# Keys and queries stored by feature with their norms folded, four unread matmuls per step, and the 64 recurrence steps written out

## The reference, cut to what matters

```
q, k, v = x@Wq, x@Wk, x@Wv            # x after a layer norm; 8 heads of 64
beta, tg = sigmoid(x@Wbeta), sigmoid(x@Wtg)   # per head and mode
qr = l2norm(rotary(q, cos, sin)) * 64**-0.5
kr = l2norm(rotary(k, cos, sin))      # angles differ by head and mode
g  = log(clip(tg * rho, 1e-6))
def step(S, inp):                     # over 512 tokens, all m, b, h
    S  = S * exp(g_t)
    dv = (v_t - k_t @ S) * beta_t
    S  = S + outer(k_t, dv)
    return S, q_t @ S
o = sum over m of softmax(mode_logits) * ys
x = x + (o * sigmoid(x@Wg)) @ Wo
x = x + experts(layernorm(x))
```

## Time and profile before

| | |
|---|---|
| median of 3 runs | 4784.18 us (4780.45 to 4792.02) |
| profiled execution, its own time | 4793.02 us |
| its span | 4790.8 us |
| mean granted TensorE clock | 0.873 of full |
| PE busy, share of the span | 4015.4 us, 84% |
| PEld | 3307.7 us, 69% |
| DVE | 3652.5 us, 76% |
| ACT | 2902.2 us, 61% |
| POOL | 371.3 us, 8% |
| DMA | 314.77 MB, mean 66 GB/s |

### The profile page before, as it was taken

One profiled execution on the slowest core, in us unless ns is written; L12 is line 12 of the kernel. 1 busy time (PEld: TensorE's weight loads), 2 busy tenths in 40 slices (PEclk: granted clock), 3 DMA queues, 4 the chain that ended last, 5 costly groups with the idle time before them and its releaser, 6 DMA issues. The chain is left out here.

```text
span 4790.8 us, 195228 instructions
## 1 busy us (share of the span) xinstructions
PE 4015.4 (84%) x85713; PEld 3307.7 (69%) x85713; DVE 3652.5 (76%) x7742; ACT 2902.2 (61%) x9736; POOL 371.3 (8%) x156
## 2 busy tenths in 40 slices
PE   5502999889988998889889988898899889987999
PEld 2201777777777777777777777777777777775666
DVE  6754888778877887788778877887788778854655
ACT  5742666666666666666666666666566666654443
POOL 1221000000000000000000000000000000000000
PEclk8755889889888998899889988998899889988999
DMA  4675222322232223222322231223122312203110
GB/s 119 167 182 133 52 51 56 83 53 52 52 87 53 52 52 87 53 52 52 87 53 52 52 87 47 57 52 87 40 59 58 82 44 58 57 10 83 36 31 7
DMA packets 283082, 314.77 MB, mean 66 GB/s; under 512 B 135768, under 2 KB 182752, under 8 KB 278112
## 3 DMA queue, kind: packets, MB, share of 16 engines
q1 hardware_dynamic: 282208, 301.99, 26.7%
HBM read 232.70 MB, written 69.21 MB: 63 GB/s over the span
## 5 line engine op out<-in xcount | busy, mean ns | idle before, releaser
L926 DVE TENSOR_TENSOR run_SC<-run_SP,run_DB 128x512 f32<-128x512 f32 x512 | 350.1, 687 | 474.6 <-PE run_SP L1057 468.3
L943 DVE TENSOR_TENSOR run_XL<-run_XL,run_EL 128x30 f32<-128x30 f32 (+14 forms) x1920 | 637.3, 332 | 66.0
L942 DVE TENSOR_TENSOR run_EL<-run_AL,run_XL 128x30 f32<-128x30 f32 (+14 forms) x1920 | 636.7, 332 | 66.0
L1053 PE MATMUL run_SP<-run_KP 64*32 64x128 f32 x8192 | 624.8, 302 | 24.5 <-DVE run_KP L901 12.7
L980 POOL TENSOR_TENSOR run_DB<-run_DB,run_below 128x2048 f32<-128x2048 f32 x64 | 297.9, 4655 | 3613.7 <-DVE run_XL L943 3487.9
L801 ACT ACTIVATE run_DB<-run_DB,run_col 128x64 f32<-128x64 f32 x2048 | 537.3, 337 | 12.0 <-POOL run_DB L980 4.2
L1053 PEld LDWEIGHTS run_SP<-run_KP 64*32 64x32 f32 x8192 | 465.6, 119 | 101.8 <-issue 50.0
L859 ACT COPY run_S<-run_KS 128x256 f32<-128x256 f32 x448 | 166.9, 373 | 556.5 <-PE run_KS L1118 556.5
L808 ACT ACTIVATE run_KD<-run_PR,run_col 128x64 f32<-128x64 f32 x2048 | 471.6, 327 | 12.9 <-PE run_PR L1073 6.8
L846 ACT ACTIVATE run_R<-run_KS,run_col 128x64 f32<-128x64 f32 x1792 | 416.0, 323 | 102.8 <-PE run_KS L1082 102.4
L1057 PE MATMUL run_SP<-run_KP 64*32 64x64 f32 x8192 | 454.5, 243 | 0.0
(11 more groups left out here) (201 smaller groups left out, 7588.8 us busy)
## 6 DMA issues: line engine op xcount, KB each, us to landing
run_DB<-G_s SPq DMA_DIRECT2D x256, 256.0 KB
run_EG<-EG_s SPq DMA_DIRECT2D x128, 512.0 KB, 8.9
run_tab<-TAB_s SPq DMA_DIRECT2D x128, 256.0 KB, 10.5
KQ_s<-proj_win SPq DMA_DIRECT2D x32, 768.0 KB, 7.8
run_win<-KQ_s SPq DMA_DIRECT2D x64, 384.0 KB, 3.1
TAB_s<-tab_tab SPq DMA_DIRECT2D x128, 128.0 KB, 2.4
run_V<-V_s SPq DMA_DIRECT2D x128, 128.0 KB, 2.6
V_s<-proj_vv SPq DMA_DIRECT2D x64, 128.0 KB, 3.1
```

The costliest lines, as they stand in the source:

```text
L942: v.link(dve.tensor_tensor(e, bcast(AL[:, r + 1:, r], 2, done), bcast(XL[:, r, 0:done], 1, rows), ALU.mult))
L943: less = dve.tensor_tensor(XL[:, r + 1:, 0:done], XL[:, r + 1:, 0:done], e, ALU.subtract)
L1053: pe.matmul(out[64 * e:64 * e + C, p].rearrange("p (z u) i -> p z (u i)", z=2), KP[f, par, p, t0:t1], KP[f, kq, p, t0:t0 + SPAN], start=Tr ...
```

## The change

**Project.** PE multiplies Wk and Wq (now the stationary operand, 128 features at a time) by all 512 tokens, so features lie on partitions. `KQ_s` holds them unscaled, by feature, with a plane for z = keys and one for queries; the rotation's negated half comes from a third product with `wn`, the negated weights. Squares are summed on PE against `pair`, two columns of ones. Instead of scaling the keys, V is multiplied by the key's norm (`root`) and the term of beta by its square; the queries' inverse norm goes to `RQ_s`, and the experts multiply the outputs by it. POOL has nothing left to do here. Each sequence's `KQ_s` is stored by 16 DMAs (before: 4), and there is one more for `RQ_s`.

**Recurrence.** `load_kq` loads `kqT` straight from `KQ_s` by 6 DMAs (1 MB) once the rotation of the pair before is done; `transposes`, `transposed`, `win` and `pe_t`, `act_t` are gone. `token_keys` uses both banks in turn. `stay_busy` is a 128x256 matmul of `ident` by `Sdec` into a half of a bank that nothing reads before it is written anew: two stand before merge(0, 0) (not in the first step), one between merge(0, 0) and merge(0, 1), and one before merge(1, 0). The tables of places move the last three token_keys one place forward and spread ACT's key copies. All 64 steps are one `emit` with constant addresses; there is no loop and no barrier within them.

**Experts.** One more DVE multiplication of 128x512 per tile of 128 tokens, 32 in all, before the one by the gate.

```diff
@@ project, store of keys and queries
-                    for i in range(NT):
-                        sp.dma_start(KQ_s[:, b, :, i, :].rearrange("h p e -> p h e"), win[:, i, :, :]).then_inc(put_k, 16)
+                    for h in range(H):
+                        at, of4 = 64 * (h % 2), 32 * (h % 4)
+                        sp.dma_start(KQ_s[h, b, :, 0:DK].rearrange("z f t -> f z t"), kf[at:at + 64, b % 2, :, h // 2, :]).then_inc(put_k[b % 2], 16)
+                        sp.dma_start(KQ_s[h, b, :, DK:].rearrange("z f t -> f z t"), nf[of4:of4 + 32, b % 2, :, h // 4, :]).then_inc(put_k[b % 2], 16)
@@ project, the products on PE
-                    pe.matmul(QB[n % 2][:, :], lhsT, wq[:, :], start=True, stop=True).then_inc(pe_q, 1)
+                    for query, w in enumerate((wk, wq)):
+                        if n:
+                            pe.wait_ge(freed[query], n)
+                        pe.matmul(FB[query][:, :], w[:, 128 * i:128 * i + 128], xT[:, b % 2], start=True, stop=True).then_inc(pe_f[query], 1)
@@ recurrence, SP
-                            sp.wait_ge(scored, SUPER * k + 2)
-                            if k + sets:
-                                sp.wait_ge(pe_t, 4 * (k + sets))
-                            load_win(n)
+                            sp.wait_ge(rot_k, NT * (k + 1))
+                            sp.wait_ge(rot_q, NT * (k + 1))
+                            load_kq(n)
@@ recurrence, merge
                             if m == 0 and k:
                                 pe.wait_ge(xt_done, 2 * k - 1)
-                                if g == 0:
-                                    pe.wait_ge(kd_done, SUPER * k)
-                                else:
-                                    pe.wait_ge(act_t, 4 * turned)
+                                pe.wait_ge(kd_done, SUPER * k)
@@ recurrence, PE
+                        def stay_busy():
+
+                            pe.matmul(KS[:, 0].rearrange("p a v -> p (a v)"), ident[:, :], Sdec[:, :, :].rearrange("p a v -> p (a v)"),
+                                      start=True, stop=True)
+
                         if runs:
+                            if k:
+                                stay_busy()
+                                stay_busy()
                             merge(0, 0)
+                            stay_busy()
                             merge(0, 1)
+                            stay_busy()
                             merge(1, 0)
-                            jobs = sc[0:1] + jobs + sc[1:] + kd[0:2] + turn[0:2] + kd[2:3] + turn[2:3] + kd[3:4] + turn[3:4]
+                            jobs = sc[0:1] + jobs + sc[1:] + kd
@@ recurrence, the order and the loop
-        PE_PLACES = [1, 2, 1, 1, 2, 1, 1, 1, 0, 0, 1, 1, 1, 1, 1, 1]
-        ACT_PLACES = [1, 1, 1, 1, 1, 1, 0, 0, 1, 1, 1, 2, 1, 1, 2, 0]
+        PE_PLACES = [1, 2, 1, 1, 2, 1, 1, 1, 0, 1, 0, 1, 0, 1, 0, 0]
+        ACT_PLACES = [1, 1, 1, 1, 1, 1, 0, 0, 1, 1, 1, 1, 1, 1, 2, 0]

         emit(-1, 0, 1, [(False, True, True)], first=True)
-        with nc.Fori(0, H - 1) as r:
-            emit(r * B, r, 0, [(True, True, True)] * B)
-        emit(NSEQ - B, H - 1, 0, [(True, True, k < B - 2) for k in range(B - 1)] + [(True, False, False)])
+        emit(0, 0, 0, [(True, True, k < NSEQ - 2) for k in range(NSEQ - 1)] + [(True, False, False)])
@@ experts, DVE
+                            heads = o[:, b % 2, i, :].rearrange("p (h v) -> p h v", h=H)
+                            dve.tensor_tensor(heads, heads, bcast(rq[:, b % 2, i, :], 2, DV), ALU.mult).then_inc(scaled, 1)
```

More of the change, by code:

```diff
@@ L156, in _ @@
                 v = Chain(dve, dve_s)
+                v.link(dve.memset(pair[:, :], 0.0))
+                for h2 in range(2):
+                    v(dve.memset(pair[64 * h2:64 * h2 + 64, h2:h2 + 1], 1.0))
                 dve.wait_ge(loaded, 11 * 16)
@@ L296, in after, with end @@
+                def end(b):
+                    square_sums(b, NT - 1)
                 def after(b, i):
+                    if b or i:
+                        pe.wait_ge(valued, NT * b + i)
+                    pe.matmul(VB[:, :, :].rearrange("p h d -> p (h d)"), xT[:, b % 2, 128 * i:128 * i + 128], wv[:, :], start=True, stop=True).then_inc(pe_v, 1)
                     if i != 2:
@@ L309, in after @@
                     last.then_inc(sums, 1)
-                in_order(begin, tile, after, lambda b: None)
+                in_order(begin, quarter, after, end)
             @block.scalar
@@ L718, in _ @@
                         load_eg(n0 + 1, (odd + 1) % 2)
-                    ran = prepared = loads = 0
+                    ran = prepared = loads = tables = 0
                     for k, (runs, prepares, more) in enumerate(steps):
@@ L762, in _ @@
                         sp.wait_ge(l_col, 16 * prepared)
-                    if first or any(more and k == 6 for k, (_, _, more) in enumerate(steps)):
-                        sp.wait_ge(l_tab, 256)
+                    if first or tables:
+                        sp.wait_ge(l_tab, 256 * max(first, tables))
                 @block.scalar
                 def _(act):
-                    token_rows = PR[0][:, :].rearrange("p (z a f) -> p z a f", z=2, a=PAIRS)
+                    token_rows = [bank[:, :].rearrange("p (z a f) -> p z a f", z=2, a=PAIRS) for bank in PR]
                     for k, (runs, prepares, more) in enumerate(steps):
@@ L807, in token_keys @@
                             for p in range(PAIRS):
-                                last = act.activation(KD[:, par, p, c, :], token_rows[:, c % 2, p, :], ACT.Copy,
+                                last = act.activation(KD[:, par, p, c, :], token_rows[c // 2 % 2][:, c % 2, p, :], ACT.Copy,
                                                       scale=col[:, par, 2, p, c:c + 1])
                             last.then_inc(kd_done, 1)
-                        if first and k == 0:
-                            for r in range(4):
-                                transposed(0, r)
                         if runs:
@@ L831, in _ @@
                             keys = [lambda c=c: token_keys(c) for c in range(SUPER)]
-                            turn = [(lambda r=r: transposed(k + sets, r)) if more else (lambda: None) for r in range(4)]
-                            jobs += ex + keys[0:4] + turn[0:2] + keys[4:6] + turn[2:3] + keys[6:8] + turn[3:4]
+                            jobs += ex + keys
                         if not runs:
@@ L1149, in _ @@
                             kd = [lambda c=c: token_keys(c) for c in range(GROUP)]
-                            wins += more
-                            turned += more
-                            turn = [(lambda r=r: transposes(k + sets, r)) if more else (lambda: None) for r in range(4)]
-                            jobs = sc[0:1] + jobs + sc[1:] + kd[0:2] + turn[0:2] + kd[2:3] + turn[2:3] + kd[3:4] + turn[3:4]
+                            jobs = sc[0:1] + jobs + sc[1:] + kd
                         if not runs:
```

277 lines of the change are left out of this document (120 added, 157 removed).

## The result

The changed kernel takes 4837.18 us (median of 4 runs, 4829.65 to 4841.33) against 4782.32 us beside it: a ratio of 1.0109, with a 95% interval of 1.009 to 1.0128. I had forecast 4465, a gain of some 320 us. The profiled execution has a span of 4827.8 us, 37 more than before.

The account below looks back on a forecast made before the run. DVE was taken to set the step and PE's clock DVE's waits. 4793.0 - 181 (ordinary steps) - 97 (loop) - 63 (tables) + 18 (rest) = 4470 us, said as 4465; range of 8 in 10: 4390 to 4640.

Parts of the forecast that it names:

- the end of an ordinary step: Recurrence: removing the turning costs nothing, a short half-rate stretch 0.9 us; steps fall from 58.2 to 54.5, 181 us in all.
- signs that I had named for a wrong forecast: Recurrence: clock staying at 0.88, ordinary steps over 56 us, or merges starting over 1 us after DVE's transposes that wait for nothing.
- The chain of the argument: Recurrence: DVE sets the step and PE's clock sets DVE's waits; full clock at the start brings 56.4 us to 53.6.
- They cost 0.2: Ordinary step: the two unread matmuls among the merges fill a gap and cost 0.2 us.
- The second price: Ordinary step: with the clock at half, the two unread matmuls among the merges cost 2.4 us.
- The rival that they are only a cost: Recurrence: clock falls despite the unread matmuls, which delay merge(1, 0) by 2.4 us per step; 4847 us, chance 0.05.
- Loop and tables: Recurrence: seven steps ending a loop pass become ordinary, 97 us; seven after a table load fall to 57.5, 63 us.
- colliding loads: Recurrence, rival: `load_kq` fills the DMA engines and stops PE; at 2 us per step 126 more, 4590 to 4700, chance 0.12.
- The rest: Outside the steps: project, first `kqT` load, experts and preparation together add 18 us.
- Project: 8 said: Project: 16 stores per sequence against 4 on SP's queue, 1 us more per sequence, 8 us; ends -15 and +60.
- Experts: 5 said: Experts: 32 more multiplications, four on the way to the first output; 5 us, between 3 and 22.
- The first load of `kqT`: Start of the recurrence: it stands before the first tables, 0.6 MB more in a queue, 3 us.

Follow-up runs that it names:

- b4: b3 with each set of turning of `win` cut from eight matmuls to one, 28 fewer per step on PE: 4731 us.
- c1: The changed kernel with six unread matmuls before merge(0, 0) in place of two, the two among the merges kept: 4738 us.
- c2: c1 with two more unread matmuls at each of PE's last three waits for ACT's W: 4602 us.
- b3: The kernel before, written out as one body and with the change's four unread matmuls, the turning of `win` kept: 4621 us.
- b2: The kernel before with the change's four unread matmuls, loop and turning of `win` kept: 4688 us.
- c4: c2 without the two unread matmuls among the merges: 4715 us.
- c5: c2 with two unread matmuls before merge(0, 0) in place of six: 4614 us.
- f2: c2 with project's 16 stores of keys and queries per sequence issued by POOL instead of SP: 4599 us.
- f3: f2 with four unread matmuls before merge(0, 0) in place of six: 4593 us.
- d1: f2 without three of four sums of squares in project from the second sequence on, and without the experts' multiplication by the queries' norms: 4571 us.
- b6: b3 with two more unread matmuls at each of PE's last three waits for W: 4713 us.
- c3: The changed kernel with only the two unread matmuls before merge(0, 0), those among the merges left out: 4746 us.
- a1: The changed kernel without its four unread matmuls per step: 4765 us.
- b1: The kernel before with its recurrence written out as one body of 64 steps, nothing else: 4720 us.
- c6: c2 with every unread matmul replaced by 20 of 32x32 by 32x32 in the same places: 5404 us.

## Why the prediction was wrong

**The step that failed** is the end of an ordinary step: "I cost their removal at nothing in an ordinary step", with "I allow for a short stretch of it in most steps, ended by the unread matmuls, at 0.9 us". Measured is 973 / 64 = 15 us at half rate per step, and an ordinary step of 59.4 us instead of 54.5. I had seen the idle time coming (some 3 us; it is 3.54 in the timeline above) and that the next step might start at half rate, and then took it, without a row to show it, that two matmuls of 0.7 us would end it. b4 and c1 to c2 show that it takes work over the end of the step: taking 28 matmuls away from b3 costs 110 us, filling PE's waits in the changed form brings 235 us (4837 to 4602). 49 x (59.4 - 54.5) = 240 of the 372 us of the miss are this. Another 45 are in the loop, 44 in the tables and 39 outside of the recurrence. Two of the signs that I had named for a wrong forecast are there: a clock over the recurrence that stays near 0.88 (0.87), and ordinary steps over 56 us (59.4).

**The chain of the argument held.** DVE sets the step and PE's clock sets its waits: in the change, b2, b3, c1, c2, c4, c5, f2, f3 and d1 the median step without any half rate lasts 54.1 to 54.9 us, and the shortest 54.1 to 54.5, where I had said 53.6. With or without the turning, by feature or by token, it is the same floor; of the kernels with a number of such steps only b6 lies above it (57.9).

**The unread matmuls.** "They cost 0.2. If their cover is gone ... 2.4". The second price is right: with the merges at half rate throughout, the way from merge(0, 0) to merge(1, 0) is 6.00 us in the change (median, 27 steps) and 3.55 and 3.56 in c3 and a1, which lack the two, so they cost 2.4. At full rate it is 3.5 us with them and 3.4 in c3, but 2.1 in c4 (63 steps): so at full rate they cost between 0.1 and 1.4, and the 0.2 holds only beside c3. I took the wrong case, full rate, for the forecast.

The rival that they are only a cost had this mechanism, a time of 4847 and a chance of 0.05. For the changed kernel it was right: the clock fell in spite of them, and without them (a1) the kernel is 72 us faster and 0.4% ahead of the kernel before. As a rule its name does not hold, since the same matmuls gain 91 and 99 us in the form before, and even in the change they took half-rate time from 1148 (a1) to 973 us. That its sum came so near is in part chance. It took 2.4 us for every ordinary step, where the merges are at half rate throughout in 27 of 64, so its ordinary step of 60.6 was 1.2 us too long (59 us in all), and the rest was 39 too small; its other terms were near, loop 54 (measured 52) and tables 28 (19).

**The Trainium skill** (TensorE: Matmul & The Clock Gate, on the clock gate) has idle gaps bring the clock down. The runs agree for idle time: with PE's waits filled, half-rate time went from 973 to 684 to 163 us. I had set this rule aside because of the earlier trace rows, and drew from them that matmuls among the merges were what was lacking. Both are needed: c4, without them, has 514 us at half rate, c3, without the filled waits, 938.

**Loop and tables.** The loop's steps ended at the length of an ordinary one, as said: b1 alone gave 60 us. I had set 97, since the ordinary step that I took was 4.9 us too short (34 us in seven steps), and since one step of 68.3 stood for a mean of 67.2. The tables' steps are 2.7 us above the ordinary ones, where I had said 3, and DVE no longer waits for `kqT`. They gave 19 and not 63: the same 34 us are missing, and one step of 66.5 stood for a mean of 64.8, which is 12 more. No sign of colliding loads: a full-rate step with `load_kq` in it lasts 54.1 us.

**The rest** was +18 and is +57. Project: 8 said, 30 measured, with my 7.5 to 19 us of SP's queue the wrong place (f2). I looked at the stores and put PE at nothing without a reason; its busy time in project rose from 135 to 226 of 295 us. Experts: 5 said, 18 measured, within the bounds: I counted the four multiplications ahead of the first output and not those of each sequence. From project's end to the tables it is 4 us more, for which I had no term. The first load of `kqT` was 3 and is 3.6 (from the first instruction of the recurrence's set-up to the first transpose, 86.2 against 82.6 us).

Open is where 18 of project's 30 us go, how much of the changed kernel's loss comes from the moved turnings of keys, and whether the clock answers to PE's busy time or to what its matmuls use of the array.

## What to carry to other kernels

Where an engine's clock depends on what it does, as PE's did here, work taken off it is not free even if it had slack: ask what the engine does in that time now, and what rate it has afterwards. Put clock-holding matmuls where the engine waits anyway; in a dependent chain they pay only if the clock really is up when it gets there, and the same two were worth +113 us and -92 us here. And read the stages around the loop with the same care as the loop: a multiplication in front of each output cost 18 us, and moving all of the added stores that I had worried about to another queue gained 4.

## What the runs showed of the hardware

- Less work for PE gave a slower kernel: 28 matmuls fewer per step lowered the mean granted clock from 0.95 to 0.89 and cost 110 us (b3, b4).
- Where the clock falls within a step matters: merge(0, 0) started at half rate in 27 of 64 steps of the changed kernel, in 8 of the kernel before, and in 1 with PE's wait ahead of it filled (c1).
- A 128x128 by 128x256 matmul in its two instructions takes 0.70 us of PE at full and 1.22 at half rate between merges.
- Matmuls of 128x128 by 128x2 take as long as their weight loads (24.0 and 24.5 us in the two rows of L301): 16 instructions take 1.84 us at full rate (from 142.25 us), 115 ns each, where the pair of 128x128 by 128x512 takes 1.02 (from 140.31). For sums over features this is a dear form: 24 of 100 us of PE in project.
- 280 matmuls of 32x32 by 32x32 in the place of 14 large ones made a step 12.6 us longer, at a mean clock of 0.83 against 0.98 (c6 against c2).
